# Expert rows moved by indirect DMA, in place of products with one-hot matrices, in a perceiver layer with a mixture of experts

## The chip, the cores and the metric

The kernel runs on one core of one Trainium2 chip. The core has a matrix engine (PE, with its weight loads listed as PEld), a vector engine (DVE), a scalar engine (ACT), GpSimd (POOL), a queue engine (SP) and 16 DMA engines. The metric is the device time of one execution in microseconds (us), as the median of several runs.

## The reference

One layer of a perceiver on x (8 batches x 64 queries x 512) and a context (8 x 1601 x 384). Between the two steps below the reference adds a self-attention whose values have the width HD - ROPE = 32 - 32 = 0; its output is zero, and the kernel leaves it out.

```python
x = x + xattn(layernorm(x), ctx, ctx, ...)        # 16 heads of 32
x = x + moe(layernorm(x), ...)

def moe(x, router_w, router_b, w1, b1, w2, b2, top_k=2):
    logits = x @ router_w + router_b              # 8 experts
    keep   = two largest logits of each token
    gating = softmax(where(keep, logits, -1e30))
    h = relu(xf @ w1[e] + b1[e])                  # 512 -> 2048
    y = h @ w2[e] + b2[e]                         # 2048 -> 512
    return sum_e y[e] * gating[:, e]
```

There are 512 tokens (T), 8 experts (E), hidden size 2048. All values are float32; the kernel splits each operand of a product into a high and a low part and takes three products ("three pass", lines 391 to 395).

## The kernel before

The first 801 us are the cross attention. What the change touches is the second part, the mixture of experts.

The part between (801 to 848 us) finishes the output projection, normalises the tokens (`xn`, 4 tiles of 128 tokens), computes the logits, the two chosen experts of each token (`keep`), the gates, and for each expert the rank of each of its tokens (`rank_e`). From the counts DVE builds a table of blocks. A block is up to 256 tokens (two tiles u = 0, 1) of one expert. A block that holds more than 128 tokens is "wide", the others are "narrow". These inputs give 8 blocks, in the order narrow, narrow, wide, wide, narrow, narrow, wide, wide.

For each block the tokens' rows are fetched with a one-hot matrix: `select` writes `sel` (tokens x 256 slots), `gather` (line 1334) multiplies the high and low half of `xn` by it, 32 matmuls of 256 columns, into the PSUM banks 4 to 7, and `gathered_high` and `gathered_low` copy the result, already turned, to `xg_hi` and `xg_lo`. The result of a block goes back with the transposed one-hot matrix: `turn_sel` (line 1399) makes it with 8 transposes, ACT and DVE take it to `sel_t` (`take_sel_t`, lines 749 and 1114), `scatter` (line 1373) multiplies it by `y_hi` and `y_lo` for each of the 4 token tiles (16 matmuls of 512 columns in a wide block, 8 in a narrow one), and DVE adds gate times product to `acc` in SBUF (line 1186). At the end SP stores `acc`.

Between lies the work of the experts. The hidden size is walked in HG = 4 groups of 512; w1 and w2 of a group are 1 MB each. SP loads them into `w_raw[g % 2]` (lines 467 to 476, the loop is 485 to 493): for group g it waits until w1 of group g is split, loads w1 of group g + 2, waits until w2 of group g is split, loads w2 of group g + 2. ACT copies each piece to `w_hi` (lines 705 to 719), DVE subtracts it to `w_lo` (lines 983 to 997).

A wide block (line 1412) walks 16 chunks c of 128 hidden units: `hidden(c)`, 12 matmuls of 256 columns, then `outputs(c - 1)`, 6 of 512 columns. ACT applies bias and ReLU (line 762), DVE makes `h_lo` (line 1133).

A narrow block (line 1444) walks the 4 groups: `hidden_group(g)`, 12 matmuls of 512 columns; the outputs of group g - 1, 12 of 512 columns; `turn_hidden(g)`, 4 transposes. ACT's order in a group is: copy `h_pre`, the two w1 pieces of group g + 2, its half of the ReLU (line 793), the two w2 pieces of group g + 1. DVE's order is: the two w2 pieces of group g (from g = 1 on), `select_next` at g = 2, its half of the ReLU (line 1168), `h_lo` (line 1173), the two w1 pieces of group g + 2; after group 3 the w2 pieces of the next block's group 0, then `y_lo`, `gathered_low` and the sums to `acc`.

All engines run their instructions in the order of the program; semaphores join them. POOL has nothing to do in the blocks.

Of the kernel before, what the change touches and what calls it, by code (L numbers as in the profile page):

```python
# [25 lines left out]
ALU = mybir.AluOpType  # L26
ACT = mybir.ActivationFunctionType
AX = mybir.AxisListType
F32 = mybir.dt.float32
# [9 lines left out]
def bass_perceiver_layer_kernel(nc, x, ctx_t, wq, bq_t, wk, bk_t, wv, bv_t, wo, bo, router_w, router_b,  # L39
# [48 lines left out]
    q_dram = nc.dram_tensor("q_scratch", (D, T), F32, kind="Internal").ap()  # L88

# [4 lines left out]
    with ExitStack() as stack:  # L94
# [110 lines left out]
        sel = place("sel", [P, TT, BLOCK], F32R, moe)  # L205
        sel_t = place("sel_t", [P, BT, T], F32R, moe)
# [15 lines left out]
        xn_hi = place("xn_hi", [P, TT, D], F32R, moe)  # L222
        xn_lo = place("xn_lo", [P, TT, D], F32R, moe)
        y_hi = place("y_hi", [P, BT, D], F32R, moe)
        y_lo = place("y_lo", [P, BT, D], F32R, moe)
# [10 lines left out]
        gate_cur = sb("gate_cur", [P, 1, TT], F32, moe)  # L236
# [19 lines left out]
        seen = sb("seen", [P, TT + 1, E], F32, moe)  # L256
        in_tile = sb("in_tile", [P, TT, E], F32, moe)
        rank1 = sb("rank1", [P, TT, E], F32, moe)
        rankk = sb("rankk", [P, TT, E], F32, moe)
# [28 lines left out]
        out_stored = sem("out_stored")  # L288
# [28 lines left out]
        counts_product, table_ready, xn_high, xn_split = sem("counts_product"), sem("table_ready"), sem("xn_high"), sem("xn_split")  # L317
# [3 lines left out]
        sel_turned, sel_t_taken = sem("sel_turned"), [sem(f"sel_t_taken{i}") for i in range(BT)]  # L321
        gather_ready, xg_high, xg_low = sem("gather_ready"), sem("xg_high"), sem("xg_low")
        h_ready, h_high, h_split = sem("h_ready"), sem("h_high"), sem("h_split")
        y_ready, y_high, y_split, scatter_ready = sem("y_ready"), sem("y_high"), sem("y_split"), sem("scatter_ready")
# [55 lines left out]
        def turned_bank(i):  # L380

            return 3 if i < 2 else 1
# [18 lines left out]
        def _(sp):  # L401
# [80 lines left out]
            load_w2(0, 1, 1)  # L482
            sp.wait_ge(table_ready, 1)
# [10 lines left out]

            for i in range(2):
                sp.wait_ge(w1_loaded[i], 16 * (HG // 2 * blocks + 1))
                sp.wait_ge(w2_loaded[i], 16 * (HG // 2 * blocks + 1))
            sp.wait_ge(y_taken, TT * (blocks + 1))
            sp.dma_start(out_rows, acc[:]).then_inc(out_stored, 16)
            sp.wait_ge(out_stored, 16)  # L500
# [3 lines left out]
        def _(pool):  # L504
# [64 lines left out]
            with pool.Fori(0, B - 1) as b:  # L569
# [18 lines left out]
                                    pattern=[[1, P]], channel_multiplier=-1).then_inc(numbers_ready, 1)  # L588


            pool.wait_ge(xn_high, 1)
            nc.gpsimd.tensor_tensor(xn_lo[:], xn[:], xn_hi[:].bitcast(F32), ALU.subtract).then_inc(xn_split, 1)
# [3 lines left out]
        def _(act):  # L596
# [135 lines left out]
            nc.scalar.copy(xn_hi[:], xn[:]).then_inc(xn_high, 1)  # L732
# [11 lines left out]
            def gathered_high(b):  # L744
                for k in range(KD):
                    act.wait_ge(gather_ready, KD * b + k + 1)
                    nc.scalar.copy(xg_hi[:, k, :], ps[:, 4 + k, 0:BLOCK]).then_inc(xg_high, 1)

            def take_sel_t(b):
                act.wait_ge(sel_turned, BT * b + 1)  # L750
                nc.scalar.copy(sel_t[:, 0, :], ps[:, 6, :]).then_inc(sel_t_taken[0], 1)
# [3 lines left out]
            with act.Fori(0, blocks) as b:  # L755
                act.wait_ge(b1_set, b + 1)
                is_wide = act.value_load(wide[0:1, bass.ds(b, 1)], min_val=0, max_val=1)
                with act.If(is_wide > 0):
                    for c in range(HT):
# [14 lines left out]
                        if c == 0:  # L774
                            take_sel_t(b)
                    w1_high_piece(HG + 1, 1, b)
                    for t in range(BT):
                        act.wait_ge(y_ready, BT * b + t + 1)
                        nc.scalar.copy(y_hi[:, t, :], ps[:, t, :]).then_inc(y_high, 1)
                with act.Else():  # L780
                    for g in range(HG):
# [5 lines left out]
                        if g == 0:  # L787
                            take_sel_t(b)
# [15 lines left out]
        def _(dve):  # L804
# [238 lines left out]
            for i in range(3):  # L1043
                nc.vector.memset(sums[i][:, 0:PAD], 0.0)
# [462 lines left out]
```

## Time and profile before

| | |
|---|---|
| median of 3 runs | 1237.94 us (1237.35 to 1240.23) |
| profiled execution, its own time | 1238.97 us |
| its span | 1237.2 us |
| PE busy | 1150.7 us, 93% |
| PEld busy | 1063.8 us, 86% |
| DVE busy | 986.2 us, 80% |
| ACT busy | 715.9 us, 58% |
| POOL busy | 425.7 us, 34% |
| DMA | 121.16 MB, mean 98 GB/s |

The page's section on the chain that ended last gives PE 80%, DVE 9%, ACT 4%, DMA 3%, issue 3%. Its slices show PE at 9 tenths in nearly all of the attention, and at 5 to 9 tenths from 770 us on. A busy share over the whole span mixes the attention with the blocks, so a change to the blocks is to be read from the stretches of the blocks. In the rows of instructions, times are microseconds from the start of the span; a bracket at the end of a row tells how long the engine was idle before it and what ended that.

### The profile page before, as it was taken

Reading aid. Unit: us, or ns where it says so; the run is one execution under the profiler, and the core shown is the slowest. Engines: PE = TensorE matmul, PEld = TensorE weight load, DVE = VectorE, ACT = ScalarE, POOL = GpSimd, SP = SyncE. Lnnn points to the kernel's source line nnn. Section 1 sums busy time; section 2 is a strip of 40 time slices with the busy share of each in tenths; the row PEclk is TensorE's granted clock in tenths of the full one; section 3 lists DMA queues with packets and bytes.
Section 4 is the critical chain, followed back from the end, with each engine's and each line's share of the span. In section 5 each row is a group of like instructions: output and inputs, shape, how many; then the busy total and the mean of one; then the engine's idle time right before and its main releaser. Section 6 shows DMA issues by size and latency. Waiting matters only on the chain.

```text
span 1237.2 us, 23354 instructions
## 1 busy us (share of the span) xinstructions
PE 1150.7 (93%) x7536; PEld 1063.8 (86%) x7537; DVE 986.2 (80%) x2130; ACT 715.9 (58%) x1482; POOL 425.7 (34%) x370
## 2 busy tenths in 40 slices
PE   5899999999999999999999998757889999889998
PEld 4799999999999999999999997635668798668897
DVE  6578898898898898899899888866786646876655
ACT  3456656656656656655665666434465555665654
POOL 5454654654654654655655540010000000000000
PEclk9899999999999999999999999967889999989999
DMA  5222122122122122121121103013754524555632
GB/s 189 91 62 62 40 69 60 38 69 60 38 69 60 38 69 60 42 67 59 44 69 55 57 23 140 26 51 110 266 199 159 187 102 170 204 202 183 203 122 102
DMA packets 74305, 121.16 MB, mean 98 GB/s; under 512 B 10776, under 2 KB 35480, under 8 KB 74272
## 3 DMA queue, kind: packets, MB, share of 16 engines
q1 hardware_dynamic: 74272, 120.73, 29.8%
q8 instruction: 20, 0.33, 0.1%
q14 instruction: 13, 0.11, 0.0%
HBM read 118.62 MB, written 2.10 MB: 98 GB/s over the span
## 4 chain that ended last, share of the span: by engine, by line
PE 80%; DVE 9%; ACT 4%; DMA 3%; issue 3%; DVEq 0%; SPq 0%; ACTq 0%
PE ps L393 18%; PE ps L394 17%; PE ps L395 17%; PE ps L1254 7%; PE ps L1294 7%; PE ps L1278 4%; PE ps L1279 3%; DMA w_raw<-in_w_dram 2%; PE ps L1340 2%; DVE w_lo L995 2%; PE ps L1256 1%; PE ps L1383 1%; DVE w_lo L987 1%; PE ps L1384 1%; DVE mx L926 1%
## 5 line engine op out<-in xcount | busy, mean ns | idle before, releaser
L522 POOL TENSOR_TENSOR ctx_hi<-ctx_raw,no_query 128x1152 fp32r<-128x1152 f32 x64 | 142.3, 2224 | 297.3 <-PE ps L395 285.8
L665 ACT ACTIVATE probs<-ps,negmax 128x1152 f32<-128x1152 f32 x64 | 78.4, 1225 | 206.3 <-DVE negmax L929 206.3
L858 DVE SCALAR_TENSOR_TENSOR k_mix<-ps,bk_sb,k_mix 64x384 fp32r<-64x384 f32 (+1 forms) x256 | 162.3, 634 | 37.6 <-ACT k_mix L620 32.9
L393 PE MATMUL ps<-wv_hi,ctx_hi 128*128 128x256 f32 (+1 forms) x624 | 181.4, 291 | 6.7 <-DVE k_mix L858 6.7
L526 POOL TENSOR_TENSOR ctx_lo<-ctx_raw,ctx_hi 128x1152 fp32r<-128x1152 f32 x64 | 179.8, 2810 | 5.0
L395 PE MATMUL ps<-wv_hi,ctx_lo 128*128 128x256 f32 (+1 forms) x624 | 175.7, 282 | 0.0
L394 PE MATMUL ps<-wv_lo,ctx_hi 128*128 128x256 f32 (+1 forms) x624 | 175.6, 281 | 0.0
L620 ACT ACTIVATE k_mix<-ps,bk_sb 64x384 fp32r<-64x384 f32 (+1 forms) x256 | 151.8, 593 | 24.0 <-PE ps L395 21.5
L940 DVE TENSOR_TENSOR pt_mix<-ps,pt_mix 128x384 fp32r<-128x384 f32 (+1 forms) x256 | 142.4, 581 | 0.3 <-ACT pt_mix L678 0.2
L393 PE MATMUL ps<-ctx_hi,wk_hi 128*128 128x384 f32 (+1 forms) x384 | 137.7, 359 | 0.0
L395 PE MATMUL ps<-ctx_hi,wk_lo 128*128 128x384 f32 (+1 forms) x384 | 132.6, 345 | 0.0
L394 PE MATMUL ps<-ctx_lo,wk_hi 128*128 128x384 f32 (+1 forms) x384 | 132.0, 344 | 0.0
L926 DVE TENSOR_REDUCE mx<-ps 128x1 f32<-128x384 f32 (+1 forms) x256 | 128.6, 565 | 0.0
L393 PEld LDWEIGHTS ps<-wv_hi,ctx_hi 128*128 128x128 f32 (+1 forms) x624 | 115.8, 186 | 8.6 <-DVE k_mix L858 8.1
L625 ACT CAST v_mix<-ps 128x256 fp32r<-128x256 f32 (+1 forms) x208 | 77.6, 373 | 75.6 <-PE ps L395 73.0
L394 PEld LDWEIGHTS ps<-wv_lo,ctx_hi 128*128 128x128 f32 (+1 forms) x624 | 116.1, 186 | 0.3
L395 PEld LDWEIGHTS ps<-wv_hi,ctx_lo 128*128 128x128 f32 (+1 forms) x624 | 115.8, 186 | 0.0
L678 ACT CAST pt_mix<-ps 128x384 fp32r<-128x384 f32 (+1 forms) x256 | 111.8, 531 | 0.6 <-PE ps L1294 0.5
L1254 PEld LDWEIGHTS ps<-pt_mix,v_mix 128*128 128x128 f32 (+1 forms) x832 | 106.7, 188 | 2.0
L1254 PE MATMUL ps<-pt_mix,v_mix 128*128 128x256 f32 (+1 forms) x832 | 108.2, 279 | 0.0
L1294 PE MATMUL ps<-ident,probs 128*128 128x128 f32 (+1 forms) x832 | 102.5, 274 | 5.9 <-ACT probs L665 5.9
L393 PE MATMUL ps<-w_hi,h_hi 128*128 128x512 f32 x192 | 81.5, 424 | 20.9 <-DVE h_lo L1173 20.8
(211 smaller groups left out, 2742.2 us busy)
## 6 DMA issues: line engine op xcount, KB each, us to landing
w_raw<-in_w_dram SPq DMA_DIRECT2D x68, 1024.0 KB, 5.2
ctx_raw<-in_ctx_t_dram SPq DMA_DIRECT2D x48, 576.0 KB, 3.8
ctx_raw<-in_ctx_t_dram SPq DMA_DIRECT2D x16, 673.5 KB, 4.1
q_both<-q_scratch SPq DMA_DIRECT2D x14, 128.0 KB, 3.0
x<-in_x_dram SPq DMA_DIRECT2D x1, 1024.0 KB, 5.1
wq_raw<-in_wq_dram SPq DMA_DIRECT2D x1, 1024.0 KB, 7.2
q_scratch<-q_out SPq DMA_DIRECT2D x1, 1024.0 KB, 5.5
wo_raw<-in_wo_dram SPq DMA_DIRECT2D x1, 1024.0 KB, 5.3
```

Source lines behind the costliest of these rows:

```text
L393: pe.matmul(acc_ap, a_hi, b_hi, start=start, stop=False)
L394: pe.matmul(acc_ap, a_hi, b_lo, start=False, stop=False)
L395: return pe.matmul(acc_ap, a_lo, b_hi, start=False, stop=stop)
L522: nc.gpsimd.tensor_tensor(ctx_hi[slot][:, :, 0:n], ctx_raw[slot][:, :, 0:n], no_query[:].rearrange("p (o i) -> p o i", o=1).broadcast_to([ ...
L526: nc.gpsimd.tensor_tensor(ctx_lo[slot][:, :, 0:n], ctx_raw[slot][:, :, 0:n], ctx_hi[slot][:, :, 0:n].bitcast(F32), ALU.subtract).then_inc( ...
L620: last = nc.scalar.activation(k_mix[rows, 2 * a + i, KEY0[c]:KEY0[c] + m], ps[rows, bank, 0:m], ACT.Identity, bias=bk_sb[rows, a:a + 1])
L678: nc.scalar.copy(pt_mix[:, TILE0[c]:TILE0[c] + n, 0, :], ps[:, SCORE_BANK + c, 0:n * P].rearrange("p (t r) -> p t r", t=n)).then_inc(pt_hi ...
L858: last = nc.vector.scalar_tensor_tensor(out=k_mix[other, 2 * a + i, cols], in0=ps[rows, bank, 0:m], scalar=bk_sb[rows, a:a + 1], in1=k_mix ...
L926: part = nc.vector.tensor_reduce(mx[:, c:c + 1], ps[:, SCORE_BANK + c, 0:KEYS[c]], AX.X, ALU.max)
L940: nc.vector.tensor_tensor(pt_mix[:, TILE0[c]:TILE0[c] + m, 1, :], ps[:, SCORE_BANK + c, 0:m * P].rearrange("p (t r) -> p t r", t=m), pt_mi ...
L1254: pe.matmul(ps[:, PV_BANK, 0:2 * P], v_mix[0:r, t, s, :, :], pt_mix[0:r, t, :, :], start=(t == 0), stop=(t == KT - 1))
L1294: last = pe.transpose(ps[0:r, SCORE_BANK + c, i * P:(i + 1) * P], probs[:, key:key + r], ident[:])
```

## The change

Rows no longer pass through products. `xn` is stored to a DRAM tensor once. For each block a small product of `sel` (now plain float32) with a table `who` of (token number, gate) gives for each slot its token's number and gate (`find_rows`, 8 matmuls of 2 columns); DVE takes them from bank 7 (`take_rows`). POOL then gathers the rows by two indirect DMAs of 128 rows of 2 KB into `xg_raw`, PE turns them (`turn_rows`, 8 transposes) and ACT and DVE split them. A block's result is multiplied by the gate (`gate_rows`, one instruction on ACT and one on DVE in a wide block; in a narrow one a memset on DVE, `no_rows`) and POOL adds it to the output in DRAM by two accumulating indirect DMAs. The sums that the gated bias and the residual give are stored to DRAM before the first block, by POOL. Slots without a token of the expert get the numbers of other tokens, each once, and the gate 0.

Moved with it: the rank and count products come before the gates' transposes; the choice of the next block (`select_next`) is at c = 4 or g = 1 instead of c = 8 or g = 2, behind `rows_in_use`, which waits for the adds of the block before; in a narrow block the hidden groups alternate between the banks 2 and 7; PE waits before hidden group 3 for `idx_ready`, since bank 7 also holds the product of `find_rows`; `gathered_high` and `gathered_low` work on halves of 512 columns, and the turning of the next block's rows comes before the last group of outputs.

```diff
+            def gather_rows(b, moved=None):
+                pool.wait_ge(xn_stored, 16)
+                pool.wait_ge(idx_ready, b + 1)
...
+                for u in range(BT):
+                    nc.gpsimd.indirect_dma_start(xg_raw[:, u, :], None, xn_dram,
+                                                 bass.IndirectOffsetOnAxis(idx_next[:, u:u + 1], 0),
+                                                 bounds_check=T - 1).then_inc(rows_moved, 16)
+            def add_rows(b, moved, all_moved):
+                pool.wait_ge(sums_stored, 16)
+                pool.wait_ge(y_taken, y_taken_by(b + 1))
+                pool.wait_ge(gate_set, b + 1)
+                pool.wait_ge(rows_moved, moved)
...
+                    nc.gpsimd.indirect_dma_start(out_flat, bass.IndirectOffsetOnAxis(idx_cur[:, u:u + 1], 0),
+                                                 y_gated[:, u, :], None, bounds_check=T - 1, compute_op=ALU.add).then_inc(rows_moved, 16)
...
+            with pool.Fori(0, blocks) as b:
+                pool.wait_ge(xg_turned, 2 * b + 2)
+                gather_rows(b + 1, moved)
+                add_rows(b, moved, all_moved)
...
+            def rows_in_use(b):
+                dve.wait_ge(idx_ready, b + 1)
+                dve.wait_ge(y_taken, y_taken_by(b))
+                dve.wait_ge(rows_moved, 64 * b + 32)
+                nc.vector.tensor_copy(idx_cur[:], idx_next[:])
+                nc.vector.tensor_copy(gate_cur[:], gate_next[:]).then_inc(gate_set, 1)
...
                     w1_low_piece(HG + 1, 0, b)
                     w1_low_piece(HG + 1, 1, b)
                     dve.sem_inc(h_relu, HG)
...
+                    gathered_low(b + 1)
+                    gate_rows(b)
                 with dve.Else():
                     for g in range(HG):
                         if g > 0:
                             for piece in range(PIECES):
                                 w2_low_piece(g, piece, b)
-                        if g == 0:
-                            take_sel_t(b)
-                        if g == 2:
+                        if g == 1:
+                            rows_in_use(b)
                             select_next(b)
+                        if g == 3:
+                            take_rows(b + 1)
...
+                    no_rows(b)
+                    gathered_low(b + 1)
...
+            def find_rows(b):
                 pe.wait_ge(sel_ready, b + 1)
+                for u in range(BT):
+                    for t in range(TT):
+                        last = pe.matmul(ps[:, 7, 2 * u:2 * u + 2], sel[:, t, u * P:(u + 1) * P], who[:, t, :],
+                                         start=(t == 0), stop=(t == TT - 1))
+                last.then_inc(idx_product, 1)
...
                 hidden(b, 0)
-                turn_sel(b)
                 for c in range(1, HT):
                     hidden(b, c)
+                    if c == HT // 2:
+                        find_rows(b + 1)
                     outputs(b, c - 1, BT)
+                turn_rows(b + 1, rows_moved_by(b))
                 outputs(b, HT - 1, BT)
-                gather_next(b, range(KD))
-                scatter(b, BT)
 
             def hidden_group(b, g):
-                if g > 0:
-                    pe.wait_ge(h_high, HT * b + 4 * g - 2)
+                if g == 3:
+                    pe.wait_ge(idx_ready, b + 2)
...
                 hidden_group(b, 0)
-                turn_sel(b)
                 turn_hidden(b, 0)
                 for g in range(1, HG):
                     hidden_group(b, g)
+                    if g == 2:
+                        find_rows(b + 1)
                     for i in range(4):
                         outputs(b, 4 * (g - 1) + i, 1)
                     turn_hidden(b, g)
-                gather_next(b, range(KD - 1))
+                turn_rows(b + 1, rows_moved_by(b))
                 for i in range(4):
                     outputs(b, 4 * (HG - 1) + i, 1)
-                gather_next(b, range(KD - 1, KD))
-                scatter(b, 1)
```

## Rows read from the trace of the kernel before

**Rows 1.** Windows: stretch, busy us of PE, PEld, DVE, ACT, POOL, clock, DMA.

```profile
801.00:848.30 47.30, 24.68 (x92) 16.95 (x92) 33.45 (x117) 16.55 (x28) 5.87 (x7) 0.66 0.27 92
891.80:932.00 40.20, 34.74 (x161) 27.74 (x162) 31.95 (x54) 23.91 (x42) 0.00 (x0) 0.92 0.58 207
932.00:986.10 54.10, 54.01 (x344) 48.47 (x344) 33.52 (x52) 31.39 (x55) 0.00 (x0) 1.00 0.54 190
1177.50:1231.80 54.30, 54.27 (x346) 48.56 (x344) 32.86 (x51) 31.39 (x55) 0.00 (x0) 1.00 0.29 97
```

**Rows 2.** Groups of instructions by line and shape, 770 to 1238 us.

```profile
L1340 PE MATMUL ps<-sel,xn_hi 128*128 128x256 f32 x144 | 24.8, 297 | 2.6 <-DVE sel L1059 2.6
L1383 PE MATMUL ps<-y_hi,sel_t 128*128 128x512 f32 x48 | 19.4, 404 | 2.5 <-DVE y_lo L1179 2.5
L1403 PE MATMUL ps<-ident,sel 128*128 128x128 f32 x64 | 9.3, 294 | 0.0
```

**Rows 3.** Timeline: plain float32 products, at the high and at a lower clock.

```profile
798.55 0.38 PE L1256 MATMUL ps<-rinv_diag,ones 128*128 128x128 f32 x2
827.09 0.64 PE L1327 MATMUL ps<-keep,before 128*128 128x32 f32 x2 [4.92 <-DVE gates L1034]
```

**Rows 4.** Timeline of the second narrow block: ACT, SP, DVE and PE around group 3.

```profile
897.34 0.58 ACT L751 CAST sel_t<-ps 128x512 fp32r<-128x512 f32 x1
904.57 0.37 SPq L476 DMA_DIRECT2D w_raw<-in_w_dram  x1
912.42 1.99 ACT L710 CAST w_hi<-w_raw 128x1024 fp32r<-128x1024 f32 x2 [5.50 <-DMA w_raw<-in_w_dram]
915.54 0.69 DVE L1173 TENSOR_TENSOR h_lo<-h_f,h_hi 128x512 fp32r<-128x512 f32 x1 [2.38 <-ACT h_hi L793]
918.42 2.35 DVE L995 TENSOR_TENSOR w_lo<-w_raw,w_hi 128x1024 fp32r<-128x1024 f32 x2
...
909.52 0.49 PE L393 MATMUL ps<-w_hi,xg_hi 128*128 128x512 f32 x1
916.28 0.79 PE L393 MATMUL ps<-w_hi,h_hi 128*128 128x512 f32 x1 [3.74 <-DVE h_lo L1173]
921.57 0.95 PE L1441 MATMUL ps<-ident,h_pre 128*128 128x128 f32 x4
923.82 0.69 DVE L1173 TENSOR_TENSOR h_lo<-h_f,h_hi 128x512 fp32r<-128x512 f32 x1
924.43 2.35 DVE L987 TENSOR_TENSOR w_lo<-w_raw,w_hi 128x1024 fp32r<-128x1024 f32 x2
926.70 2.35 DVE L995 TENSOR_TENSOR w_lo<-w_raw,w_hi 128x1024 fp32r<-128x1024 f32 x2
931.83 0.38 PE L393 MATMUL ps<-xg_hi,w_hi 128*128 128x256 f32 x1
```

**Rows 5.** Windows: PE at its low clock in the same block.

```profile
916.00:920.00 4.00, 3.72 (x9) 2.94 (x10) 4.00 (x5) 2.93 (x5) 0.00 (x0) 0.50 0.52 203
```

**Rows 6.** Timeline: ends of two wide blocks and the start of the next.

```profile
978.04 2.35 DVE L987 TENSOR_TENSOR w_lo<-w_raw,w_hi 128x1024 fp32r<-128x1024 f32 x2
989.14 0.38 PE L393 MATMUL ps<-xg_hi,w_hi 128*128 128x256 f32 x1 [2.89 <-issue]
...
1179.02 0.17 DVE L1125 COPY b_cur<-b_sb 128x16 f32 x1 [0.49 <-issue]
1179.98 0.47 ACT L762 ACTIVATE h_f<-ps,b_cur 128x256 f32<-128x256 f32 x1 [5.55 <-DVE b_cur L1125]
```

**Rows 7.** Timeline: PE's first product after the last outputs.

```profile
1224.05 0.65 PE L1340 MATMUL ps<-sel,xn_hi 128*128 128x256 f32 x4
```

**Rows 8.** DMA issues of the whole span: KB each, median us to landing.

```profile
q_both<-q_scratch SPq DMA_DIRECT2D x14, 128.0 KB, 3.0
out_dram<-acc SPq DMA_DIRECT2D x1, 1024.0 KB, 4.2
```

**Rows 9.** Timeline: PE's first product of the first block.

```profile
848.37 0.79 PE L393 MATMUL ps<-w_hi,xg_hi 128*128 128x512 f32 x1 [5.55 <-issue]
```

More of the change, by code:

```diff
@@ L204, in bass_perceiver_layer_kernel @@
         xt_lo = place("xt_lo", [P, KD, T], F32R, moe)
-        sel = place("sel", [P, TT, BLOCK], F32R, moe)
-        sel_t = place("sel_t", [P, BT, T], F32R, moe)
+        sel = place("sel", [P, TT, BLOCK], F32, moe)
+        xg_raw = place("xg_raw", [P, BT, D], F32, moe)
         xg_hi = place("xg_hi", [P, KD, BLOCK], F32R, moe)
@@ L493, in _ @@
                     load_w2(owner_next, (g + 2) % HG, g % 2)
[L495 to L500, printed above, removed]
+            sp.wait_ge(xn_stored, 16)
+            sp.wait_ge(sums_stored, 16)
         @block.gpsimd
@@ L595, in _ @@
+            for i in range(2):
+                pool.wait_ge(w1_loaded[i], 16 * (HG // 2 * blocks + 1))
+                pool.wait_ge(w2_loaded[i], 16 * (HG // 2 * blocks + 1))
+            pool.wait_ge(rows_moved, all_moved)
         @block.scalar
@@ L744, in gathered_high, with gate_rows @@
             def gathered_high(b):
[L745 to L751, printed above, removed]
+                for half in range(2):
+                    act.wait_ge(xg_turned, 2 * b + half + 1)
+                    nc.scalar.copy(xg_hi[:, 2 * half:2 * half + 2, :],
+                                   ps[:, 4 + half, :].rearrange("p (k s) -> p k s", k=2)).then_inc(xg_high, 1)
+            def gate_rows(b):
+                act.wait_ge(y_ready, BT * b + 1)
+                act.wait_ge(gate_set, b + 1)
+                act.wait_ge(rows_moved, rows_moved_by(b))
+                nc.scalar.activation(y_gated[:, 0, :], ps[:, 0, :], ACT.Identity, scale=gate_cur[:, 0:1]).then_inc(y_taken, 1)
             gathered_high(0)
@@ new lines, in gate_rows, with no_rows @@
+            def gate_rows(b):
+                dve.wait_ge(y_ready, BT * b + 2)
+                dve.wait_ge(gate_set, b + 1)
+                dve.wait_ge(rows_moved, rows_moved_by(b))
+                nc.vector.tensor_scalar(y_gated[:, 1, :], ps[:, 1, :], gate_cur[:, 1:2], None, ALU.mult).then_inc(y_taken, 1)
+            def no_rows(b):
+                dve.wait_ge(rows_moved, rows_moved_by(b))
+                nc.vector.memset(y_gated[:, 1, :], 0.0).then_inc(y_taken, 1)
+            select(0, rank_e[:, 0:1, :], 0.0, gates_e[:, 0, :])
```

228 lines of the change are left out of this document (112 added, 116 removed).

## The prediction

> **What bounds the kernel now.** I read the busy times by stretch first [rows 1]. The attention before 801 us is not touched. The routing part, 801 to 848.3, leaves every engine idle for much of its time and PE at 0.66 of its clock: it is a chain of small steps. In the wide blocks (932 to 986.1, 1177.5 to 1231.8) PE is busy for 54.0 of 54.1 and 54.3 of 54.3 us, so PE's own work is their time. In the narrow block 891.8 to 932 PE is busy 34.7 of 40.2 us, DVE 32.0, ACT 23.9, and the clock averages 0.92: no engine is full, so the order of the waits decides. The timeline of that block [rows 4] shows them. SP can issue the loads of w2 group 3 and w1 group 4 only at 904.57, when DVE has split w2 of group 1. ACT stands 5.50 us for the landing of the latter, until 912.42, makes `w_hi` and only then its part of the ReLU. DVE's `h_lo` follows at 915.54, and PE, idle for 3.74 us, starts the outputs of group 2 at 916.28. PE had run hidden group 3 long before, from 909.52 on, and that is the fact on which my forecast turns.
>
> **What the change takes from PE and gives to it.** The busy times of pipelined products overlap, so I count the distances of their starts. Of the gather's, four together last 0.65 us [rows 7] with 0.29 for one [rows 2], so they start 0.12 apart: 32 x 0.12 = 3.8 us in any block. Products of 512 columns start (921.57 - 916.28)/12 = 0.44 apart at half the clock [rows 4, 5], so 0.22 to 0.23 at the full one, and the scatter's 16 are 3.7 us in a wide block, its 8 are 1.9 in a narrow one [rows 2]. Turning `sel` is 8 transposes 0.11 apart [rows 2, 3], 0.9, and turning the gathered rows costs the same 0.9 again. `find_rows` is new: 8 plain float32 products, each two instructions in the trace. Two such instructions last 0.38 with 0.27 for one, so they start 0.11 apart at the high clock; at the clock of the routing part the distance is 0.64 - 0.41 = 0.23 [rows 3]. The 2 columns are fewer than in either row, but the weights are 128 columns in both: 16 x 0.11 to 0.12 = 1.9 us in a block (ends 0.9, if half of it goes with the columns, and 3.7, at the low clock). PE's work thus shrinks by 3.8 + 3.7 - 1.9 = 5.6 us in a wide block, by 3.8 in a narrow one.
>
> **Narrow blocks.** Follow the block that starts at 891.86. ACT's copy of `sel_t`, 0.58 at 897.34, goes, and everything behind it comes 0.5 earlier: SP's issue at 904.1, `h_lo` of group 2 at 915.1 [rows 4]. Then comes the new wait. PE may not start hidden group 3 before `idx_ready`, and DVE gives that in `take_rows`, which is queued at g = 3 behind `h_lo` of group 2, the w1 pieces of group 4 and the w2 pieces of group 3. DVE's pair of w2 pieces started at 918.42 and takes 2.35 [rows 4]; less 0.5, plus two copies of 0.2 (as the small copy of [rows 6]), `idx_ready` is at 920.7. So hidden group 3 moves from 909.52 to 920.75, behind the landing of the weights, where it had been hidden in ACT's wait. Behind it on PE are queued the outputs of group 2, the turn of group 3, the turned rows and the outputs of group 3; ACT's `h_pre` and SP wait for them.
>
> The sum from there. Hidden group 3 is 12 products, 0.23 apart at the high clock and 0.43 at the low one. PE will have been idle for some 10 us. [...] I take 5.0: 925.75. The outputs of group 2 take 2.75 at the high clock: 928.5. The 4 transposes of the turn take 0.35: 928.9. From that turn's end to the end of `h_lo` it is 924.51 - 922.27 = 2.2 [rows 4], which covers the 0.9 of the turned rows: 931.1. The outputs of group 3, 2.75, end at 933.85. But DVE has, behind `h_lo`, the pairs of 924.43 and 926.70, 2.3 us each, then the memset of `no_rows` (at most 0.3), and then `gathered_low`, 0.7 for its first half: 931.05 + 4.6 + 0.3 + 0.7 = 936.7. The next block's first product stood at 931.83 [rows 4] and now waits for that. **+4.9 us in a narrow block**, four times: +19.6. The select, moved to g = 1, delays the ReLU of group 1 by 2 us, but PE waits 10 us behind it anyway; if that cover were gone it would cost 2.
>
> **Wide blocks.** At the block's end DVE splits two w1 pieces from 978.04 to 980.39 [rows 6], and `gathered_low` is queued behind them. PE, with turned rows before the last outputs, would be ready at 979.2; it waits for the first half, 980.4 + 0.1 + 0.7 = 981.2, instead of starting the next block at 986.1: -4.9. `find_rows` adds 1.9, no `turn_sel` takes 0.9. A new wait comes at the next start: ACT's first ReLU needs `b1_cur`, 0.96 behind DVE's copy [rows 6], and DVE copies it after `gathered_low` and `gate_rows`. From wide to wide that is some 2 us after PE's start, the ReLU and `h_lo` 2.3 later, and PE is there at 2.9: 1.5 of wait; from narrow to wide, with no `gate_rows` on DVE, 0.6. The third block began behind 2.89 us of "issue" [rows 6]; if that stays it runs beside the wait for `xg_low`, and the start is 982.2 in place of 989.14, -6.9. So: first wide block -6.9 + 1.9 - 0.9 + 0.6 = -5.3; second -4.9 + 1.9 - 0.9 + 1.5 = -2.4; third -3.3. The last one has until the end of its outputs +1.9 - 0.9 + 1.5 + 0.9 - 0.4 = +3.0. Its tail was 1237.2 - 1224.05 = 13.15 [rows 7]. Now: 3.3 until DVE's `gate_rows`, 0.8 for two issues, the landing, 0.4 for the end. No accumulating or indirect DMA stands in the trace; the pair moves 0.5 MB to a destination that is also read, so it lies between 3.0 (128 KB) and, with all reads and writes apart, twice the 4.2 of 1 MB [rows 8]. I take 4.2: 8.7, so -4.4 (ends -5.6 and 0). All wide blocks: -5.3 - 2.4 - 3.3 + 3.0 - 4.4 = **-12.4**.
>
> **Where DMAs hide.** The gather of a narrow block is issued at 921 and wanted at 929, with 3 us more before it delays the next start; in a wide block it has 20 us. The adds have 11 to 13 us until `rows_in_use`. Against a landing of 3.0 to 8.4 [rows 8] both cost nothing; without cover they cost what exceeds those. The add lies beside the loads of the next w1 group 3, which then lands up to 4 us later, and ACT's wish for it moved by as much.
>
> **Routing part.** The rank product comes earlier, with 16 small instructions 0.23 apart [rows 3]; `sel` is ready when it was. `find_rows` takes 3.7 there in place of 6.4 of gather, but then stand `take_rows`, the gather (2.4 to 6 with its issues), the turned rows and the split, and DVE's table comes 4 us later. The first product at 848.37 stood behind 5.55 us of "issue" [rows 9] that follow its last wait, and the new last wait falls within 1 us of the old. I take **+1** (ends -1 and +4).
>
> **The clock.** New idle times of PE, 2.9 us before the next start behind a narrow block and 2 behind a wide one, follow on a block's half that was mostly idle. If the first hidden products then run at 0.50 [rows 5] they cost 2.4 in each of 4 and 1.3 in each of 3 places, 0 to 13.6. I take 5.
>
> **Sum.** 19.6 - 12.4 + 1 + 5 = +13.2, on the span 1237.2: 1250.4. Around the span lie 1.8, and the profiled execution was 1.0 above the median: 1251.
>
> **Rivals.** (A) Forecast: 1251; own range 1243 to 1263. (B) Faster: the wait for `idx_ready` costs nothing, because DVE's pieces come earlier than I have it or the group's landing does. The narrow block would then be bounded by DVE's two pairs behind `h_lo` of 923.8 [rows 4]: 924.0 + 4.6 + 0.3 + 0.7 = 929.6 against 931.83, -2.2 each. Time: 1238 - 8.8 - 12.4 + 1 = 1218. For it speaks PE's smaller work; against it the order of the two programs, which leaves DVE no other place. (C) About the same: the mechanism is there but PE comes to the high clock early in hidden group 3 (-2 each) and loses nothing elsewhere: 1251 - 5 - 8 = 1238. [...]
>
> **Chances.** A 0.58, B 0.17, C 0.10, D 0.15. The range 1234 to 1275 leaves out B and the far part of D. A measurement of this kernel can tell 0.3%, 3.7 us, from no change: faster 0.17, same 0.10 (C), slower 0.73 (A and D).
>
> **What would show it.** In a narrow block: hidden group 3 starts behind `idx_ready`, with 8 to 11 us of idle PE before it, at 0.5 of the clock, and the block takes 44 to 47 us in place of 40. In a wide block: PE waits some 2 us for `xg_low` at the end and 0.6 to 1.5 for the first `h_lo`, and the block takes 50 to 52. `turn_rows` and `rows_in_use` wait for no DMA. I am wrong if hidden group 3 follows the turn of group 2 directly (B), or if PE or DVE stands for `rows_moved` (D).

## The result and the profile after

| | before | after |
|---|---|---|
| median of 4 runs | 1238.45 us (1237.35 to 1240.23) | 1251.41 us (1248.95 to 1252.46) |
| profiled execution, its own time | 1238.97 us | 1251.24 us |
| its span | 1237.2 us | 1249.4 us |
| DVE busy | 986.2 us | 954.1 us |
| POOL busy | 425.7 us | 467.5 us |

After to before is 1.010, 95% interval 1.0084 to 1.0117: the change made the kernel slower by 1.0%. The prediction was 1251 us, range 1234 to 1275. The first section of the page of the changed kernel (busy us and share of each engine):

```profile
PE 1120.0 (90%) x7316; PEld 1034.5 (83%) x7317; DVE 954.1 (76%) x2096; ACT 705.9 (56%) x1451; POOL 467.5 (37%) x406
```

PE works 30.7 us less than before, and the kernel takes 12 us more (a span of 1249.4 in place of 1237.2). The windows of the second narrow block and of the first and third wide ones, beside those of [rows 1] (stretch, length, busy us of PE, PEld, DVE, ACT, POOL with their instructions, granted clock, DMA share, GB/s):

```profile
899.78:944.54 44.76, 30.15 (x137) 23.54 (x137) 28.60 (x51) 23.48 (x39) 5.36 (x4) 0.89 0.63 211
944.54:994.63 50.09, 48.30 (x312) 43.60 (x312) 27.79 (x46) 30.01 (x51) 5.35 (x4) 1.00 0.64 196
1136.11:1186.20 50.09, 48.30 (x313) 43.60 (x313) 27.80 (x46) 30.02 (x51) 5.37 (x4) 1.00 0.64 196
```

In the narrow block PE, DVE and ACT each do less than before (30.2, 28.6 and 23.5 us in place of 34.7, 32.0 and 23.9), POOL has 5.4 us of new work, and the block is longer: it got more waiting, not more work. In the wide blocks PE's work fell from 54 to 48.3 us, and 1.8 us of new waiting stand beside it. The waits of the changed kernel (engine, its tile and line, what ended the wait, us in total, times, longest):

```profile
PE ps L412 <- DVE gate_next L1119: 39.6, 4, 10.2
ACT w_hi L765 <- DMA w_raw<-in_w_dram: 22.2, 4, 5.7
PE ps L412 <- DVE xg_lo L1133: 15.6, 7, 2.6
PE ps L1430 <- DMA xg_raw<-xn_scratch,idx_next: 1.5, 3, 0.7
PE ps L412 <- DVE h_lo L1214: 0.7, 2, 0.4
```

The first line is the wait for `idx_ready`, once in each narrow block; the third the wait for the split rows, once before every block but the first. The timeline of the second narrow block, the same place as [rows 4] (start, length, and in brackets the idle time and what ended it; first ACT and DVE, then PE):

```profile
919.99 1.99 ACT L765 CAST w_hi<-w_raw 128x1024 fp32r<-128x1024 f32 x2 [5.57 <-DMA w_raw<-in_w_dram]
923.11 0.69 DVE L1254 TENSOR_TENSOR h_lo<-h_f,h_hi 128x512 fp32r<-128x512 f32 x1 [2.30 <-ACT h_hi L846]
923.72 2.35 DVE L1039 TENSOR_TENSOR w_lo<-w_raw,w_hi 128x1024 fp32r<-128x1024 f32 x2
925.99 2.35 DVE L1047 TENSOR_TENSOR w_lo<-w_raw,w_hi 128x1024 fp32r<-128x1024 f32 x2
928.33 0.15 DVE L1119 COPY gate_next<-ps 128x2 f32<-128x2 f32 x1
...
928.62 0.79 PE L412 MATMUL ps<-w_hi,xg_hi 128*128 128x512 f32 x1 [9.88 <-DVE gate_next L1119]
936.27 0.60 PE L1502 MATMUL ps<-ident,h_pre 128*128 128x128 f32 x4
937.40 1.09 PE L1430 MATMUL ps<-ident,xg_raw 128*128 128x128 f32 x8 [0.53 <-DMA xg_raw<-xn_scratch,idx_next]
938.91 0.50 PE L412 MATMUL ps<-w_hi,h_hi 128*128 128x512 f32 x1 [0.42 <-DVE h_lo L1254]
944.54 0.39 PE L412 MATMUL ps<-xg_hi,w_hi 128*128 128x256 f32 x1 [2.57 <-DVE xg_lo L1133]
```

ACT still stands 5.57 us for its weights, `h_lo` of group 2 follows, and only behind that and four weight pieces does DVE copy the numbers of the next rows. PE's hidden group 3, which ran during ACT's wait before, starts at 928.62, 28.84 us into the block in place of 17.66.

All kernels of this study are compared block by block below. Each number is the distance from a block's first product to the next block's, read from PE's timeline; the last wide block counts to the start of its last product, and the tail from there to the end of the span. N is narrow, W wide, in the order of execution.

| kernel (profiled execution) | first block at | N1 | N2 | W1 | W2 | N3 | N4 | W3 | W4 | tail |
|---|---|---|---|---|---|---|---|---|---|---|
| before | 848.4 | 43.5 | 40.0 | 57.3 | 55.5 | 39.0 | 39.8 | 54.2 | 46.2 | 13.4 |
| after | 850.4 | 49.4 | 44.8 | 50.1 | 50.4 | 45.4 | 45.6 | 50.1 | 48.3 | 14.9 |
| e1, numbers taken early | 847.3 | 42.1 | 38.9 | 50.1 | 50.4 | 38.8 | 38.6 | 50.1 | 48.3 | 14.6 |
| e2, group 3 in bank 2 | 851.4 | 48.7 | 44.8 | 50.0 | 50.4 | 43.4 | 44.0 | 50.0 | 48.3 | 15.0 |
| e3, rows split first | 851.1 | 45.8 | 43.9 | 52.1 | 50.5 | 42.4 | 46.1 | 52.2 | 50.3 | 14.6 |
| e4, e1 and e3 | 849.4 | 40.3 | 38.9 | 48.8 | 51.9 | 39.1 | 38.2 | 49.2 | 50.3 | 14.9 |
| e5b, no adds | 848.6 | 48.9 | 44.6 | 50.1 | 50.4 | 45.4 | 45.6 | 50.1 | 48.3 | 5.8 |
| e6, plain stores | 846.5 | 49.1 | 44.5 | 50.1 | 50.4 | 45.4 | 47.8 | 52.5 | 49.2 | 11.8 |
| e7, e1 and a new wide end | 852.3 | 43.2 | 38.4 | 48.4 | 49.0 | 38.8 | 38.8 | 48.2 | 48.8 | 12.8 |
| e8, e7 and the ReLU first | 849.6 | 37.3 | 33.5 | 49.4 | 49.0 | 35.0 | 35.1 | 48.2 | 48.8 | 13.3 |
| e9, before with the ReLU first | 850.8 | 37.3 | 34.6 | 57.5 | 56.6 | 34.6 | 34.6 | 54.2 | 46.2 | 13.4 |
| e10, e8 and a new narrow end | 849.6 | 35.1 | 36.4 | 48.4 | 49.0 | 33.8 | 31.1 | 48.4 | 48.8 | 13.0 |

From before to after the four narrow blocks together take 23.0 us more, the wide ones 14.3 less, the tail 1.5 more, and the first block starts 2.0 later: together the 12.2 us between the spans.

### The profile page after: what moved, and what is told of

The parts are those of the page before. It is cut to its first block, busy times and chain, and to the rows that moved or that the text cites. A ratio compares the mean times of both kernels' runs of the same rounds, so it can differ in the third digit from the quotient of the medians.

```text
span 1249.4 us, 22923 instructions
## 1 busy us (share of the span) xinstructions
PE 1120.0 (90%) x7316; PEld 1034.5 (83%) x7317; DVE 954.1 (76%) x2096; ACT 705.9 (56%) x1451; POOL 467.5 (37%) x406
## 4 chain that ended last, share of the span: by engine, by line
PE 77%; DVE 9%; issue 5%; ACT 4%; DMA 3%; DVEq 1%; SPq 0%; ACTq 0%; POOL 0%; POOLq 0%
PE ps L412 18%; PE ps L413 17%; PE ps L414 17%; PE ps L1327 7%; PE ps L1367 7%; PE ps L1351 4%; PE ps L1352 3%; DMA w_raw<-in_w_dram 2%; DVE w_lo L1047 2%; DVE w_lo L1039 1%; PE ps L1329 1%; PE ps L1419 1%; DVE mx L978 1%; DVE pt_mix L992 1%; DVE k_mix L910 1%
## 5 line engine op out<-in xcount | busy, mean ns | idle before, releaser
L617 POOL DMA_INDIRECT xg_raw<-xn_scratch,idx_next x18 | 19.5, 1081 | 231.4 <-DVE gate_next L1119 228.7
```

## Experiments

The theory is that DVE's late `take_rows` is the loss: hidden group 3 waits for it and leaves its cover. The rivals are that the time was lost anyway to ACT's wait for weights, and that POOL's DMAs take it. Times are medians of 4 to 10 runs; the kernel before, run again beside them, gave 1238 to 1240 us.

### Taking the numbers early (e1)

```diff
-                        if g == 3:
+                        if g == 2:
                             take_rows(b + 1)
                         dve.wait_ge(h_ready, HT * b + 4 * g + 4)
```

> Of the changed kernel, only DVE's take_rows in a narrow block moves from g = 3 to g = 2, ahead of its part of the ReLU. The changed kernel's trace shows PE idle 9.8 to 10.2 us before hidden group 3 in each of the four narrow blocks, ended by DVE's gate_next. Theory A (this wait is the loss, because DVE gives idx_ready only behind h_lo of group 2 and four weight pieces): the wait ends behind the w2 pieces of group 2, before h_lo of group 2, so hidden group 3 falls back into ACT's wait for its weights; a narrow block takes 38 to 41 us in place of 45.3, the four give 18 to 29 us, and the kernel takes 1222 to 1233. Rival R1 (the idle time was only moved there: the landing of the w1 load of group g + 2 bounds the narrow block, as the 5.50 us on ACT in the kernel before suggest): the 10 us disappear before group 3 but return before h_lo of group 2, a block keeps 44 to 45 us, and the kernel stays at 1247 to 1251.

Measured: 1221.96 us, 0.986 of the kernel before (0.9838 to 0.9883), 29 us below the changed kernel. A narrow block takes 38.6 to 38.9 us (the first 42.1); the wide blocks and the tail stay within 0.3 us, and the start is 3.1 earlier. In the timeline of its second narrow block:

```profile
909.21 0.15 DVE L1118 CAST idx_next<-ps 128x2 uint32<-128x2 f32 x1
909.28 0.15 DVE L1119 COPY gate_next<-ps 128x2 f32<-128x2 f32 x1
909.35 1.99 ACT L765 CAST w_hi<-w_raw 128x1024 fp32r<-128x1024 f32 x2 [5.29 <-DMA w_raw<-in_w_dram]
909.57 0.49 PE L412 MATMUL ps<-w_hi,xg_hi 128*128 128x512 f32 x1 [1.29 <-DVE gate_next L1119]
910.33 1.09 POOL L617 DMA_INDIRECT xg_raw<-xn_scratch,idx_next  x1 [17.16 <-DVE gate_next L1119]
```

The wait of 9.9 us is one of 1.3, and hidden group 3 stands beside ACT's wait for its weights again. The theory holds, and the rival that ACT's wait for weights loses the same time anyway falls. (Of the 30 us between the two profiles, 26.9 are in the narrow blocks.)

### Another bank for group 3 (e2)

```diff
-            return 2 if g % 2 == 0 else 7
+            return 7 if g == 1 else 2
...
-                    pe.wait_ge(idx_ready, b + 2)
+                    pe.wait_ge(h_high, HT * b + 4 * g - 2)
```

> Of the changed kernel, hidden group 3 of a narrow block goes to bank 2 in place of 7 and waits for ACT's h_pre of group 2 (as in the kernel before) in place of idx_ready; take_rows stays at g = 3. This takes the wait away and leaves the order of DVE alone. Theory A: narrow blocks take 37 to 41 us; idx_ready comes at the same distance behind h_lo of group 2, so earlier than now by what that h_lo comes earlier, and the gather still has some cover. The kernel takes 1222 to 1233, within 4 us of the run with the early take_rows. A variant of A: the gather of the next rows is still issued late (behind take_rows at g = 3), PE stands 2 to 4 us in each narrow block for xg_raw before the last outputs, and the kernel takes 1230 to 1240, 8 us or more above the early take_rows. Rival R1 (weights bound the block anyway): 1247 to 1251.

Measured: 1247.38 us. I expected 1222 to 1240, and only 4 us of the 29 came. By its number this run lies at the edge of what I had given the rival of the weights (1247 to 1251); e1 has refuted that rival, and the waits of this kernel show another cause:

```profile
PE ps L1430 <- DMA xg_raw<-xn_scratch,idx_next: 40.7, 4, 11.2
PE ps L412 <- DVE h_lo L1254: 10.8, 7, 2.4
```

And its timeline at the first narrow block:

```profile
884.20 0.15 DVE L1119 COPY gate_next<-ps 128x2 f32<-128x2 f32 x1
885.22 1.07 POOL L617 DMA_INDIRECT xg_raw<-xn_scratch,idx_next  x1 [30.16 <-DVE gate_next L1119]
886.59 1.09 POOL L617 DMA_INDIRECT xg_raw<-xn_scratch,idx_next  x1 [0.30 <-issue]
893.69 1.97 PE L1430 MATMUL ps<-ident,xg_raw 128*128 128x128 f32 x8 [10.51 <-DMA xg_raw<-xn_scratch,idx_next]
```

The wait on PE is gone, and PE stands at the gathered rows instead: from the end of the copy of the gates to the first turned row it is 9.3 us, of which 0.9 to the first issue, 1.4 to the second and 7.1 from there. So the wait instruction is not the loss. The lateness of the numbers is, and it has two customers, PE's bank and the gather; freeing one shows the other. The variant that I had written down, 2 to 4 us of such a wait in each narrow block, had the place right and the size at a third: it is 40.7 us in four. In the changed kernel the gather was nearly hidden only because hidden group 3 and the outputs of group 2 stood behind the same event (PE waits 0.3 to 0.7 us for it there).

### Splitting the rows before the weight pieces (e3), and both (e4)

```diff
+                    gathered_low(b + 1)
                     w1_low_piece(HG + 1, 0, b)
                     w1_low_piece(HG + 1, 1, b)
                     dve.sem_inc(h_relu, HG)
-                    gathered_low(b + 1)
                     gate_rows(b)
```

(and the same on ACT and in narrow blocks)

> Of the changed kernel, gathered_high and gathered_low go ahead of the weight pieces of the block's end, on ACT and DVE, in both kinds of block: the wait for idx_ready stays. The trace of the changed kernel shows PE waiting 1.76 us three times and 2.6 us four times for xg_lo, 15.6 us in all, behind DVE's pieces. Theory A (these waits are a loss of their own, on top of that for idx_ready): they go, but the pieces come later by the 1.3 us of the split, so some of it returns at the next group; 1237 to 1243. Rival R2 (PE comes earlier to the next block but stands there for weights or for the ReLU instead, so the wait only moves): 1248 to 1252.

> The early take_rows and the early split of the rows together. If the two losses are independent, their gains add: 1251 less 18 to 29 less 8 to 14, so 1208 to 1225, faster than the kernel before by 1 to 2.5%. If both were paid out of the same slack (the narrow block is then bounded by its weight loads or by DVE's 32 us of work), the sum falls short by 5 us or more, and the kernel takes 1222 to 1230.

Measured: e3 1251.13 us, e4 1224.03 us. Neither is faster than the kernel it is built on. The 15.6 us of waits for `xg_lo` are gone in e3, and the time is not: PE's waits for the first `h_lo` of a wide block went from 0.7 to 10.1 us, those for ACT's `h_pre` from 4.3 to 9.4. DVE, ACT and PE at the start of W2 in e3:

```profile
993.14 2.35 DVE L1040 TENSOR_TENSOR w_lo<-w_raw,w_hi 128x1024 fp32r<-128x1024 f32 x2
995.41 0.74 DVE L1144 TENSOR_SCALAR y_gated<-ps,gate_cur 128x512 f32<-128x512 f32 x1
996.07 0.17 DVE L1209 COPY b_cur<-b_sb 128x16 f32 x1
997.02 0.47 ACT L820 ACTIVATE h_f<-ps,b_cur 128x256 f32<-128x256 f32 x1 [3.10 <-DVE b_cur L1209]
998.45 0.49 PE L412 MATMUL ps<-w_hi,h_hi 128*128 128x512 f32 x1 [2.49 <-DVE h_lo L1215]
```

PE starts the block earlier and meets the first ReLU, which waits for the block's bias; DVE copies that behind the weight pieces and the gate. The chain at a block's end is DVE's whole queue (rows, pieces, gate, bias); a permutation in which PE needs the last of it moves the wait and no more. The table shows it: in e3 the wide blocks are together 6.2 us longer, W1, W3 and W4 by 2 each, and the narrow ones together 7.0 shorter. e4 fell into the case of one slack that pays for both (1222 to 1230).

### What the adds cost (e5b, e6)

```diff
-                for u in range(BT):
-                    nc.gpsimd.indirect_dma_start(out_flat, bass.IndirectOffsetOnAxis(idx_cur[:, u:u + 1], 0),
-                                                 y_gated[:, u, :], None, bounds_check=T - 1, compute_op=ALU.add).then_inc(rows_moved, 16)
```

> Of the changed kernel, the two accumulating DMAs of each block are left out, so the experts' part never comes into the output; the gathers and all else stay, and the counts that were waited for are made smaller to fit. Theory T (the adds are hidden in the blocks and cost only the tail, 14.6 us from the end of the last outputs, of which the two adds with their landing are some 10.5): every block keeps its time within 0.3 us and only the tail shrinks, to some 4 us, so 1239 to 1243. Rival D' (the adds also take bandwidth from the weight loads, or hold POOL and through it DVE up): the blocks shrink too, narrow ones by 1 us or more, and the time is 1236 or less.

> Of the changed kernel, the adds become plain indirect stores (no accumulation), so the output holds the last expert's part of each token in place of the sum. It prices the accumulation alone. If reading the destination is what makes the landing 6.6 us, it falls to some 4 (a plain store of 1 MB took 4.2 before) and the time to 1248 to 1250. If the price is that of 128 separate rows with an index each, landing stays at 6 to 7 us, POOL's 1.6 us stays, and the time stays at 1250 to 1252. If POOL's 1.6 us against the gather's 1.1 is for the accumulation, it falls to 1.1 (two times 0.5 off the tail).

Measured: without adds 1239.63 us, 11.8 below the changed kernel. Seven blocks keep their time within 0.15 us, the first is 0.5 shorter, and the tail falls from 14.9 to 5.8; the first block started 1.8 earlier in this execution, which is no part of the adds. The adds are hidden in the blocks, and 9.1 us of the tail are theirs.

With plain stores: 1248.11 us, and the tail is 11.8. In this profile the last blocks have a lower clock than in the changed kernel (0.82 in place of 0.86 in N4, 0.97 in place of 1.00 in W3, both 2 us longer), so I read only the tail from it. POOL's rows at the end, first of the changed kernel:

```profile
1238.73 1.63 POOL L629 DMA_INDIRECT out_dram<-y_gated,idx_cur  x1 [23.07 <-DVE y_gated L1143]
1240.66 1.59 POOL L629 DMA_INDIRECT out_dram<-y_gated,idx_cur  x1 [0.30 <-issue]
```

then with plain stores:

```profile
1239.68 1.03 POOL L629 DMA_INDIRECT out_dram<-y_gated,idx_cur  x1 [23.16 <-DVE y_gated L1143]
1241.02 1.02 POOL L629 DMA_INDIRECT out_dram<-y_gated,idx_cur  x1 [0.30 <-issue]
```

and the landings of these two in each (a view of the DMAs from 1236 us on), the changed kernel first:

```profile
out_dram<-y_gated,idx_cur POOLq DMA_INDIRECT x2, 5.1
```

```profile
out_dram<-y_gated,idx_cur POOLq DMA_INDIRECT x2, 2.8
```

Accumulating costs 0.6 us of POOL for each of these two DMAs (1.63 and 1.59 in place of 1.03 and 1.02) and 2.3 us of landing; 1.2 + 2.3 = 3.5 against the 3.1 by which the tail is shorter.

### A new end of the wide block (e7)

On top of e1. DVE copies the next block's bias behind the gate, and the last w1 pieces come behind both; ACT's last piece stands behind its gate.

```diff
-                    w1_low_piece(HG + 1, 0, b)
-                    w1_low_piece(HG + 1, 1, b)
                     dve.sem_inc(h_relu, HG)
                     gathered_low(b + 1)
                     gate_rows(b)
+                    next_b1(b + 1)
+                    w1_low_piece(HG + 1, 0, b)
+                    w1_low_piece(HG + 1, 1, b)
```

> On top of the early take_rows: at the end of a wide block ACT and DVE split the gathered rows and apply the gate before the last w1 pieces, and DVE copies the next block's first bias right behind them, so that what returned in the run with the rows first (PE 2.5 us behind a late bias) has no cause. Theory A: three waits of 1.76 us go, the wait for the first h_lo stays under 0.5, and the tail loses 2.3 us since the gate no longer stands behind two weight pieces: 1222 - 5.3 - 2.3 = 1214 (1212 to 1217). Rival (the wait moves again, to h_lo behind the w1 pieces or to a later load): only the tail's 2.3 us is gained, 1219 to 1221.

Measured: 1216.09 us, 5.9 below e1. Its five runs fall into two groups, three at 1215.6 to 1216.1 and two at 1220.4 to 1220.6; the profiled one is of the second, and its first block starts at 852.3, 5.0 later than in e1. The blocks are the better measure: W1, W2 and W3 take 48.2 to 49.0 us in place of 50.1 to 50.4, together 5.0 less, and the tail is 1.8 shorter, against the 5.3 and 2.3 that I had expected. This is what e3 lacked: with the bias, too, in front of the pieces, little of the gain comes back (0.5 us in W4).

A part of what the tail lacks, 0.34 us of 0.5, has a cause that I had overlooked. In e7 the first add of the last block took POOL 1.97 us, in the changed kernel 1.63. It now starts while DVE splits a weight piece, which in the changed kernel no add does. The part on rival D below says more. The row of e7:

```profile
1208.13 1.97 POOL L629 DMA_INDIRECT out_dram<-y_gated,idx_cur  x1 [20.99 <-DVE y_gated L1143]
```

### The ReLU before the w1 pieces (e8), in the kernel before too (e9)

In narrow blocks, on ACT (DVE's pieces follow in the same order):

```diff
-                        for piece in range(PIECES):
-                            w1_high_piece(g + 2, piece, b)
                         act.wait_ge(h_ready, done + 4)
...
                         for piece in range(PIECES):
                             w2_high_piece(g + 1, piece, b)
+                        for piece in range(PIECES):
+                            w1_high_piece(g + 2, piece, b)
```

> On top of that, in narrow blocks ACT makes its part of the ReLU and the w2 pieces before the w1 pieces of group g + 2, whose landing it now waits for (4.0 to 5.3 us per group in the run with the early take_rows), and DVE's pieces follow in the same order. If that wait on the path is what bounds the narrow block now, PE's waits for h_lo (3.0, 2.0 and 3.0 us in a block) go, and four blocks give 4 times 4 to 8 us: 1182 to 1200. If DVE's 32 us of work and the gather's 9 us from index to rows bound it, 1204 to 1212. If the weights' loads bound it (8 MB in 38.8 us), 1212 to 1216.

> The kernel before the change, with the same reorder as in the last run (in a narrow block ACT makes the ReLU and the w2 pieces before the w1 pieces of group g + 2, DVE's pieces follow). If ACT's wait for its weights bounded the narrow block of the kernel before (5.50 us on ACT, 3.74 us on PE), four blocks give 3 to 5 us each: 1218 to 1228; the mended changed kernel at 1202 then still lies 16 to 26 us below it, which is what the change is worth in an order that suits it. If the narrow block of the kernel before was bounded by something else (PE's own order, DVE's pairs before gathered_low), it stays at 1234 to 1240.

Measured: e8 1202.02 us, e9 1221.29 us (0.9855 of before, 0.984 to 0.987). The narrow blocks fall by 4 to 6 us in e8, and by 4.3 to 6.2 in e9. In the stretch of the blocks ACT waited 26.6 us for weights before and 36.1 in e1; in neither e8 nor e9 is such a wait among ACT's longer ones. Before, ACT's ReLU stood behind the landing of weights that are wanted two groups later. That is a loss of the old kernel which the change did not touch. It was also the cover under which hidden group 3 ran. My numbers for e8 missed: 1202 lies between the case of ACT's wait (1182 to 1200) and that of DVE and the gather (1204 to 1212). Both are there. Among what remains on PE in e8:

```profile
PE ps L412 <- DVE xg_lo L1133: 8.9, 4, 2.9
PE ps L1431 <- DMA xg_raw<-xn_scratch,idx_next: 5.3, 3, 2.6
PE ps L412 <- DVE h_lo L1254: 1.9, 2, 1.5
```

### A new end of the narrow block (e10)

```diff
                         for piece in range(PIECES):
                             w2_low_piece(g + 1, piece, b)
+                        if g == HG - 1:
+                            no_rows(b)
+                            gathered_low(b + 1)
+                            next_b1(b + 1)
                         for piece in range(PIECES):
                             w1_low_piece(g + 2, piece, b)
-                    no_rows(b)
-                    gathered_low(b + 1)
-                    next_b1(b + 1)
```

(ACT's `gathered_high` likewise)

> On top of the run with the ReLU first (1202): at the end of a narrow block too, the gathered rows are split and the next bias is copied before the w1 pieces. PE's waits for xg_lo there are 1.5, 2.9, 2.6 and 1.9 us. If they are a loss of their own, now that the bias is no longer late: 1194 to 1198. If the work only moves behind the next start again, as it did in the run with the rows first: 1200 to 1203.

Measured: 1193.77 us, 0.9637 of the kernel before (0.9624 to 0.965). The last two blocks before the final wide one (N4 and W3), as windows:

```profile
1052.26:1083.33 31.07, 27.54 (x137) 21.94 (x136) 27.49 (x49) 23.09 (x39) 5.94 (x4) 1.00 0.87 293
1083.33:1131.70 48.37, 48.16 (x313) 43.80 (x313) 28.02 (x46) 29.84 (x52) 6.35 (x4) 1.00 0.63 199
```

These two are near PE's own work, at a clock of 1.00: PE is busy for 27.5 of 31.1 us in the narrow block and for 48.2 of 48.4 in the wide one. N4 is the shortest of the narrow blocks; the other three take 33.8 to 36.4 us, at a clock of 0.90 to 0.91, and still hold waits. I had expected 1194 to 1198. Of the 44.7 us (3.6%) below the kernel before, 17.2 are to be had without the change (e9). The same reorder is not all that separates e9 and e10, since e10 also has the new block ends; what is shown is that the moved rows, in an order made for them, end at 1194, and the products with one-hot matrices, with the one reorder tried on them, at 1221.

## Why the prediction was right, point by point

The mechanism came true, and the sum came out better than its terms. Against the 13.2 us that I had added to the span, 12.2 were measured: the narrow blocks were 3.4 more than I had, the wide ones 6.3 less, the tail 5.9 more, the start 1.0 more, and the 5 for the clock are already inside the measured blocks. That these errors cancel to 1 us is luck. The direction is not: the narrow blocks cost 23.0 us against the 14.3 that the wide ones save.

**The narrow block: the mechanism and the times.** I had the block's events at these distances from its first product: `idx_ready` 28.9, end of group 3 at 33.9, the turn at 36.6, the last outputs at 39.2, the next block at 44.8. The second narrow block shows 28.7 (the copy ends at 928.48), 33.7 (the next product starts at 933.51), 36.5, 39.1 and 44.8. For the 12 products of group 3 I had taken 5.0, near the 0.43 from start to start at the low clock, and for that clock the 0.50 that stands behind 3.74 us of idle time in the kernel before [rows 4, 5]. Here the idle time is 9.88 us, and the window of group 3 in that block shows 0.59:

```profile
928.60:934.00 5.40, 5.38 (x15) 4.25 (x16) 0.00 (x0) 0.23 (x1) 2.16 (x2) 0.59 0.78 259
```

and its 12 products took 4.9 us against my 5.0 (5.2, 5.3 and 4.5 in the other three narrow blocks), so rival C, with 2 us less in each, is refuted; in e1, behind 1.29 us of idle time and at a clock of 1.00, it is 3.7 from the first of them to the next product, 0.62 of it a wait. So +4.9 became +4.8 there. The size was off in the other three, at +5.9, +6.5 and +5.8: I had multiplied the one block by four, and three of the four have other lengths before (43.5, 39.0, 39.8 in place of 40.0) while those of N3 and N4 after are alike within 0.9 us of N2. My sum of 19.6 measured 23.0.

**The wide blocks: right in sign, low in size.** Predicted -5.3, -2.4, -3.3 and +3.0, together -8.0; measured -7.2, -5.1, -4.1 and +2.0, together -14.3. Three terms account for 5.6 of the 6.3. The wait at the next start from wide to wide was 0.37 us in place of 1.5, since `b_cur` came 1.1 us behind PE's start and not 2 (both times, PE's row of the first outputs has [0.37 <-DVE h_lo L1214]); behind narrow blocks no such wait stands in place of my 0.6. The 2.89 us of "issue" before W2 [rows 6] are gone whole, where I had 2.0 of them gone. And W2 of the kernel before had a clock of 0.97 behind that gap and took 1.3 us more than W3; after, it has 1.00. I had not looked at the clock of that block. The terms of PE's work itself stand: 54.0 us became 48.3, that is -5.7 against my -5.6 for what was removed and added. `find_rows` measured 1.84 to 1.89 us against my 1.9.

**The tail: the term that failed.** I had -4.4 and the tail grew by 1.5, outside my bounds of -5.6 and 0. The step was the two issues at 0.4 each and the landing of 4.2, for which I had only rows of plain DMAs that SP issues [rows 8]. Measured from the end of the last outputs (1234.87): 2.96 until the gate is applied (mine 3.3), 0.90 to POOL's first issue, 3.52 for two instructions of POOL, and 7.15 from there to the end of the span, 14.5 in place of 8.7. The two adds occupied POOL for 1.63 and 1.59 us with 0.30 between them, and that was on the path. The error of 5.9 here and that of 6.3 in the wide blocks went against each other, and with them the sum came closer than its terms deserve.

**The clock.** I had 5 us for low clock behind the new waits at block starts. The window 1090.48 to 1093.5, the start of N4, shows 0.51; the starts of N2, N3 and the four wide blocks show 1.00. So it is one place of seven, some 2.4 us by my own price, and that is inside the +5.8 of N4.

**Routing and start.** I had +1, measured +2.0 at the first block. But the same instructions of the attention reached one product, which waits for `k_mix`, at 35.59 us before and at 38.70 after, so 3.1 us arise in the first 39 us, in which nothing was changed, and the routing part is 1.1 shorter. In the profiles of e1, e4, e6, e8 and e10 that product stands at 35.4 to 35.9, in e2, e3 and e5b at 37.4 to 38.6: it varies from execution to execution. e9 shows it best, since it has the instructions of the kernel before up to its first narrow block: a later product of the attention, at 46.54 us before, stands there at 48.93. What makes the difference stays open. In the sum these 3.1 us took the place of the clock's 5.

**DMAs hidden in the blocks: right.** e5b shows the adds cost the blocks nothing. The gather exceeded its cover by 0.3 to 0.7 us in narrow blocks; I had said that PE waits for no DMA. But the cover was an accident of the same lateness, as e2 shows; I had counted 8 us of cover without asking what would be left of it if PE's wait were gone.

**Rival B** asked what happens if the wait costs nothing, and gave 1218 us; e1 makes that case and measured 1222. **Rival D**, to which I gave 0.15, was that POOL's DMAs land late. The upper end of my range, 1275, is 1251 with 3 us more in each of 8 blocks. No run shows those 3 us, an estimate of mine; e5b shows that without the adds seven blocks keep their time within 0.15 us and the first is 0.5 shorter. D did not decide this kernel: its 16 adds took POOL 1.57 to 1.63 us each and landed after a median of 6.6 us, its 18 gathers after 3.7. But adds that hold POOL longer exist. In the changed kernel no add begins while DVE splits a weight piece, so these 16 say nothing about it. In the kernels with a new wide end some do. The rows of e10 at the start of W3:

```profile
1083.86 2.35 DVE L1040 TENSOR_TENSOR w_lo<-w_raw,w_hi 128x1024 fp32r<-128x1024 f32 x2
1085.09 2.62 POOL L629 DMA_INDIRECT out_dram<-y_gated,idx_cur  x1 [9.79 <-ACT y_gated L809]
1088.02 1.59 POOL L629 DMA_INDIRECT out_dram<-y_gated,idx_cur  x1 [0.30 <-issue]
```

The first add starts beside the second of DVE's two pieces and takes 2.62 us; the second starts with DVE at work on no piece and takes 1.59. The first ends at 1087.71, 1.50 behind the piece's end at 1086.21. In e7, e8 and e10 together 15 adds began while such a piece ran. They took 1.73 to 2.62 us, and every one ended 1.49 to 1.50 us behind the end of that piece. None of the other 113 adds in the traces took more than 1.63. Gathers show the same: eight in e2, e4, e8 and e10 began 0.45 us or more before the end of a running piece or `h_lo`, took 1.40 to 1.98 us in place of 1.07, and ended 0.90 to 0.94 behind it. So in these traces the end of POOL's instruction keeps its distance from the end of DVE's subtraction, 1.5 us for an add and 0.9 for a gather. What joins the two is not shown, and no run was made to test it. The price was at most 1.0 us for a DMA; W3 of e10, with the add of 2.62 us at its start, took 48.4 us against 48.2 in e7 and e8; in the tail of e7, e8 and e10 it is 0.35 us.

## What to carry to other kernels

Ask of every result that a change makes on a busy engine who waits for it and what is queued before it: here two copies of 0.15 us behind four weight pieces cost 29 us and turned a gain of 16 (e1) into a loss of 13, and taking one customer's wait away (e2) gave back 4 of them. In these runs, putting one item of a block's end first moved the wait (e3), and putting all that the next block needs before the prefetch work removed most of it (e7, e10). Price the tail of an accumulating indirect DMA by itself, since nothing covers it there (14.9 us here, 5.8 without the adds), and look at what DVE runs when such a DMA is issued (1.6 us on POOL in the changed kernel, up to 2.62 beside a weight piece in e10). When times in one trace speak against a rival, check that what the rival asks for occurs in it: none of the 16 adds of the changed kernel began beside a weight piece.

## What the hardware showed that I had not expected

- An indirect DMA of 128 rows of 2 KB held POOL for a median of 1.07 us as a gather (changed kernel), for 1.00 to 1.03 as a plain scatter (e6) and for 1.57 to 1.63 as an accumulating scatter (changed kernel), with 0.30 us between two of them. Among those that began while DVE subtracted one SBUF tile from another, an add held it for 2.62 us (e10) and a gather for 1.98 (e8). In the tail, with no other DMA beside the pair, the plain scatters landed in 2.8 us and the accumulating ones in 5.1.
- The landing of the same gather was 3.4 us at best and 6.7 at worst over the 18 of the changed kernel, with a median of 3.7; the pair of a narrow block, beside two weight loads of 1 MB, took 5.8 to 6.1, that of a wide one 3.4 to 3.6.
- The "issue" gap before W2 of the kernel before (2.89 us) stands in e9 too (3.04 us), and in no kernel with the change. What it is stays open.
